# Two graph layers on one core: the attention weight as the larger of two exponentials instead of the exponential of a sum

## The reference

```python
def layer0(A, X, W, b):                       # X: normalised, rectified x
    idx = first 25 neighbours of each node by number
    agg = X[idx].max(axis=neighbours)          # and 0, where a node has 25 or fewer
    return relu(concat([X, agg]) @ W + b)

def layer1(inp, adj, W, a):
    h = inp @ W
    s1, s2 = h @ a[:256], h @ a[256:]
    e = leaky_relu(s1[:, :, None] + s2[:, None, :], negative_slope=0.4)
    att = softmax(where(adj > 0, e, -1e20), axis=1)
    return gelu(att @ h)

x = x + layer0(adj, relu(layernorm(x)), W0, b0)
x = x + layer1(relu(layernorm(x)), adj, W1, a)
```

## Time and profile before

| | us |
|---|---|
| median of three runs | 4289.62 |
| the three runs | 4287.83 to 4291.81 |
| the profiled execution | 4290.73 |
| its span on the core | 4288.9 |
| DVE busy | 3346.5 |
| POOL busy | 3107.7 |
| PE busy | 2657.1 |
| ACT busy | 1947.6 |

### The profile page before, as it was taken

One profiled execution on the slowest core, in us unless ns is written; L12 is line 12 of the kernel. 1 busy time (PEld: TensorE's weight loads), 2 busy tenths in 40 slices (PEclk: granted clock), 3 DMA queues, 4 the chain that ended last, 5 costly groups with the idle time before them and its releaser, 6 DMA issues. The chain is left out here.

```text
span 4288.9 us, 43562 instructions
## 1 busy us (share of the span) xinstructions
PE 2657.1 (62%) x13568; PEld 2016.8 (47%) x13568; DVE 3346.5 (78%) x7253; ACT 1947.6 (45%) x2108; POOL 3107.7 (72%) x3205
## 2 busy tenths in 40 slices
PE   2333356666666666675676666666666666666669
PEld 2222234554445454454454554455445554454547
DVE  5666689966898669986799767996689876998656
ACT  4223255532665236642366335553255532664146
POOL 5777777777777777777777777777777777777730
PEclk8555557677777777777767777777776777677779
DMA  6555556666666766666666766666666666566531
GB/s 216 166 167 173 174 183 216 209 221 212 208 213 206 232 212 197 218 221 223 203 216 204 226 222 206 213 199 225 213 211 217 210 225 218 188 218 202 172 114 55
DMA packets 412749, 860.09 MB, mean 201 GB/s; under 512 B 67299, under 2 KB 248422, under 8 KB 396134
## 3 DMA queue, kind: packets, MB, share of 16 engines
q0 software_dynamic: 153600, 419.64, 32.0%
q1 hardware_dynamic: 258918, 437.67, 30.2%
HBM read 714.43 MB, written 142.61 MB: 200 GB/s over the span
## 5 line engine op out<-in xcount | busy, mean ns | idle before, releaser
L410 POOL DMA_INDIRECT gb<-h_table,idx x3200 | 3107.0, 971 | 1009.2 <-issue 962.2
L965 PE MATMUL ps_av<-hz,lk 128*128 128x256 f32 x3712 | 1136.1, 474 | 179.1 <-DVE hz L805 179.1
L965 PEld LDWEIGHTS ps_av<-hz,lk 128*128 128x128 f32 x3712 | 891.4, 247 | 418.9 <-issue 256.6
L724 DVE TENSOR_REDUCE hl<-gb 128x256 f32<-128x3328 f32 x128 | 740.8, 5787 | 401.6 <-DMA gb<-h_table,idx 401.2
L724 DVE TENSOR_REDUCE gb<-gb 128x256 f32<-128x3328 f32 x128 | 748.5, 5847 | 10.9 <-DMA gb<-h_table,idx 10.9
L1018 PE MATMUL ps_t<-cf,hl 128*128 128x128 f32 x512 | 121.1, 382 | 694.2 <-DVE hl L724 694.2
L1023 PE MATMUL ps_l<-w,hcat 128*128 128x256 f32 x1024 | 461.1, 628 | 86.5 <-ACT hcat L538 86.5
L538 ACT COPY hcat<-ps_t 128x512 f32<-128x512 f32 x128 | 74.9, 585 | 864.9 <-PE ps_t L1018 864.5
L1036 PE MATMUL ps_t<-cf,y 128*128 128x128 f32 x256 | 72.2, 375 | 586.7 <-ACT y L551 586.7
L1018 PEld LDWEIGHTS ps_t<-cf,hl 128*128 128x128 f32 x512 | 79.3, 192 | 740.8 <-issue 740.8
L426 ACT ACTIVATE sg<-ps_c 128x2048 bf16<-128x2048 bf16 x128 | 240.1, 1876 | 410.3 <-PE ps_c L942 399.3
(11 more groups left out here) (128 smaller groups left out, 3555.9 us busy)
## 6 DMA issues: line engine op xcount, KB each, us to landing
ad<-in_adj SPq DMA_DIRECT2D x128, 1024.0 KB
p_rest<-lk SPq DMA_DIRECT2D x112, 512.0 KB, 3.4
lk<-p_rest SPq DMA_DIRECT2D x112, 512.0 KB, 3.9
gb<-h_table,idx POOLq DMA_INDIRECT x3200
edges_t<-stage SPq DMA_DIRECT2D x32, 1024.0 KB, 7.1
edge<-edges_t SPq DMA_DIRECT2D x64, 512.0 KB, 7.0
xl<-in_x SPq DMA_DIRECT2D x128, 128.0 KB
hl<-h_table SPq DMA_DIRECT2D x128, 128.0 KB
```

Of the source, the lines that this page charges most:

```text
L410: pool.indirect_dma_start(gb[c][:, s + (c > 0), :], None, table[tb], bass.IndirectOffsetOnAxis(idx[u][:, k:k + 1], 0)).then_inc(gathered[c ...
L724: V.tensor_reduce(dst, gb[c][:, :, :].rearrange("p k c -> p c k"), AX.X, ALU.max).then_inc(maxed[c], 1)
L965: ins = T.matmul(accumulator(k), lk_of(jj, u, drain)[:, k * P:(k + 1) * P], hz[jj][:, :], start=False, stop=False)
```

## The change

The leaky rectifier is the larger of x and 0.4 x, and the exponential grows with its argument; so the weight is the larger of two exponentials. ACT now computes exp(val + s2 + bias) into `lk`, and exp(0.4 val + bias) in place over `val` (`exps`). DVE takes the larger of the two in pieces of 512 and sums them with an accumulator per piece, `z_p` (`item_max`); `item_rows` sums the four. Both biases must stand before the exponentials, so `item_bounds` runs per item, right behind its values, with one instruction more, and `take_s2` moves ahead of the first values. What waited for `exp_ready` (PE, the store, `item_rows`) or `leaky_ready` (the next values in the same tile) now waits for `p_ready`, the maximum on DVE. `BLOCKED` becomes a power of two.

```diff
@@ ACT
-            def relu_part(i, j, jj, u, drain):
-                act.wait_ge(S["val_ready"], firsts(i) + 1)
+            def exps(i, j, jj, u, drain):
+                act.wait_ge(S["bounds_ready"], firsts(i) + 1)
                 act.wait_ge(S["av_done"], i - 2 if drain else i)
                 act.wait_ge(p_stored[jj], min(firsts(i) // 2, (NB - 1) * PAIRS) * 16)
-                nc.scalar.activation(lk_of(jj, u, drain)[:, :], val[jj][:, :], ACT.Relu, scale=1 - SLOPE,
-                                     bias=s2p[:, bass.ds(j, 1)]).then_inc(S["relu_ready"], 1)
-
-            def exp_part(i, j, jj, u, drain):
-                act.wait_ge(S["leaky_ready"], firsts(i) + 1)
-                bias, q = nb[:, bass.ds(j, 1)], lk_of(jj, u, drain)
-                nc.scalar.activation(q[:, :], q[:, :], ACT.Exp, bias=bias, accum_out=za[:, bass.ds(j, 1)]
-                                     ).then_inc(S["exp_ready"], 1)
+                nc.scalar.activation(lk_of(jj, u, drain)[:, :], val[jj][:, :], ACT.Exp, bias=nb[:, 1, bass.ds(j, 1)])
+                nc.scalar.activation(val[jj][:, :], val[jj][:, :], ACT.Exp, scale=SLOPE, bias=nb[:, 0, bass.ds(j, 1)]
+                                     ).then_inc(S["exps_ready"], 1)
...
-                if rest and not drain:
-                    exp_part(it - 2, j2, 0, 1 - u, drain)
                 if rest:
-                    relu_part(it - 1, j1, 1, 1 - u, drain and t > 0)
-                if rest and drain:
-                    exp_part(it - 2, j2, 0, 1 - u, drain)
+                    exps(it - 1, j1, 1, 1 - u, drain and t > 0)
...
-                if rest and not (drain and new):
-                    exp_part(it - 1, j1, 1, 1 - u, drain)
...
-                    relu_part(it, j, 0, u, drain)
-                if rest and drain and new:
-                    exp_part(it - 1, j1, 1, 1 - u, drain)
+                    exps(it, j, 0, u, drain)
@@ DVE
-            def item_bounds(o, i, j):
-                dve.wait_ge(S["val_ready"], firsts(i) + 2)
+            def item_bounds(o, i, j, jj):
+                dve.wait_ge(S["val_ready"], firsts(i) + 1)
...
+                dve.wait_ge(order, n)
+                V.tensor_tensor(nb[:, 1, bass.ds(j, 1)], nb[:, 0, bass.ds(j, 1)], s2p[:, bass.ds(j, 1)], ALU.add
+                                ).then_inc(S["bounds_ready"], 1)
...
-                    ins = V.scalar_tensor_tensor(out=q[:, p:p + PIECE], in0=val[jj][:, p:p + PIECE], scalar=SLOPE,
-                                                 in1=q[:, p:p + PIECE], op0=ALU.mult, op1=ALU.add)
-                ins.then_inc(S["leaky_ready"], 1)
+                    k = p // PIECE
+                    ins = V.scalar_tensor_tensor(out=q[:, p:p + PIECE], in0=q[:, p:p + PIECE], scalar=1.0,
+                                                 in1=val[jj][:, p:p + PIECE], op0=ALU.mult, op1=ALU.max,
+                                                 accum_out=z_p[:, jj, k:k + 1])
+                ins.then_inc(S["p_ready"], 1)
...
-                    dve.wait_ge(S["exp_ready"], firsts(i) + 1)
+                    dve.wait_ge(S["p_ready"], firsts(i) + 1)
+                    n = o.mark(V.tensor_reduce(za[:, bass.ds(j, 1)], z_p[:, jj, :], AX.X, ALU.add))
+                    dve.wait_ge(order, n)
                     n = o.mark(V.reciprocal(rz[:, bass.ds(j, 1)], za[:, bass.ds(j, 1)]))
```

More of the change, by code:

```diff
@@ L46 @@
 SLOPE = 0.4
-BLOCKED = 1e30
+BLOCKED = 2.0 ** 100
 PIECE = 512
@@ L153, in graph_layers @@
         m_a = sb("m_a", [P, 2, 2], fp32)
-        nb = sb("nb", [P, TILES], fp32)
+        nb = sb("nb", [P, 2, TILES], fp32)
+        z_p = sb("z_p", [P, 2, N // PIECE], fp32)
         za = sb("za", [P, TILES], fp32)
@@ L774, in item_value @@
                 ins.then_inc(S["val_ready"], 1)
-            def item_bounds(o, i, j):
-                dve.wait_ge(S["val_ready"], firsts(i) + 2)
+            def item_bounds(o, i, j, jj):
+                dve.wait_ge(S["val_ready"], firsts(i) + 1)
                 dve.wait_ge(order, o.n)
-                n = o.mark(V.tensor_reduce(m_t[:, :], m_p[:, :, :], AX.X, ALU.max))
+                n = o.mark(V.tensor_reduce(m_t[:, 0:1], m_p[:, jj, :], AX.X, ALU.max))
                 dve.wait_ge(order, n)
-                o.mark(V.tensor_scalar(m_a[:, 1, :], m_t[:, :], -SLOPE, None, ALU.mult))
-                n = o.mark(V.scalar_tensor_tensor(out=m_a[:, 0, :], in0=m_t[:, :], scalar=SLOPE - 1,
-                                                  in1=s2n[:, bass.ds(j, 2)], op0=ALU.mult, op1=ALU.add))
+                o.mark(V.tensor_scalar(m_a[:, 1, 0:1], m_t[:, 0:1], -SLOPE, None, ALU.mult))
+                n = o.mark(V.scalar_tensor_tensor(out=m_a[:, 0, 0:1], in0=m_t[:, 0:1], scalar=SLOPE - 1,
+                                                  in1=s2n[:, bass.ds(j, 1)], op0=ALU.mult, op1=ALU.add))
@@ L785, in item_bounds @@
                 dve.wait_ge(order, n)
-                o.mark(V.scalar_tensor_tensor(out=nb[:, bass.ds(j, 2)], in0=m_a[:, 0, :], scalar=0.0,
-                                              in1=m_a[:, 1, :], op0=ALU.min, op1=ALU.add))
-            def item_leaky(o, i, jj, u, drain):
+                n = o.mark(V.scalar_tensor_tensor(out=nb[:, 0, bass.ds(j, 1)], in0=m_a[:, 0, 0:1], scalar=0.0,
+                                                  in1=m_a[:, 1, 0:1], op0=ALU.min, op1=ALU.add))
+                dve.wait_ge(order, n)
@@ L791, in item_leaky, with item_max @@
+                V.tensor_tensor(nb[:, 1, bass.ds(j, 1)], nb[:, 0, bass.ds(j, 1)], s2p[:, bass.ds(j, 1)], ALU.add
+                                ).then_inc(S["bounds_ready"], 1)
+            def item_max(o, i, jj, u, drain):
                 q = lk_of(jj, u, drain)
-                dve.wait_ge(S["relu_ready"], firsts(i) + 1)
+                dve.wait_ge(S["exps_ready"], firsts(i) + 1)
                 for p in range(0, N, PIECE):
-                    ins = V.scalar_tensor_tensor(out=q[:, p:p + PIECE], in0=val[jj][:, p:p + PIECE], scalar=SLOPE,
-                                                 in1=q[:, p:p + PIECE], op0=ALU.mult, op1=ALU.add)
@@ L847, in step @@
                         take_s1(o, b)
+                        take_s2(o, b)
+                        dve.wait_ge(S["s_copied"], b)
                     if not sweep:
                         item_value(o, it, j, 0, drain)
+                        item_bounds(o, it, j, 0)
                 if old and drain and not before:
-                    item_leaky(o, it - 1, 1, 1 - u, drain)
+                    item_max(o, it - 1, 1, 1 - u, drain)
                 if old:
@@ L858, in step @@
                 if old and not drain and not before:
-                    item_leaky(o, it - 1, 1, 1 - u, drain)
-                if new and not t:
-                    take_s2(o, b)
+                    item_max(o, it - 1, 1, 1 - u, drain)
                 if words:
@@ L893, in step @@
                     item_value(o, it + 1, j + 1, 1, drain)
-                if new and sweep == 0:
-                    if not t:
-                        dve.wait_ge(S["s_copied"], b)
-                    item_bounds(o, it, j)
+                    item_bounds(o, it + 1, j + 1, 1)
                 if new and drain:
-                    item_leaky(o, it, 0, u, drain)
+                    item_max(o, it, 0, u, drain)
                 if old and t:
```

10 lines of the change are left out of this document (4 added, 6 removed).

## The result

| | us |
|---|---|
| before, median of 4 runs | 4290.28 (4287.83 to 4291.81) |
| after, median of 4 runs | 4321.42 (4316.75 to 4326.44) |
| ratio, 95% interval | 1.0072 (1.006 to 1.0084) |
| profiled execution of after, and its span | 4319.31, 4317.5 |

The change makes the kernel 31 us slower, 0.7%. The forecast was 13 us slower (4303): the direction is right, but the size is less than half of the loss. The time lies above the forecast's own range of 4290 to 4317 and inside the wider one of 4280 to 4330. The two spans differ by 4317.5 - 4288.9 = 28.6 us.

What follows compares the result with a forecast made beforehand. POOL sets the pace until the drain, with DVE as full in attention steps. 4290.7 us plus 12 uncovered DVE time plus 1.9 drain, less 1.1 for the median, gave 4303; own range 4290 to 4317, wider 4280 to 4330.

Steps and rivals of the forecast that it cites:

- The size of the addition: DVE in attention steps: bounds, sum and maximum add 1.5 us per step, 10.5 us per round.
- a halved maximum: Rival on DVE: each maximum piece takes twice 0.61 us, giving 4561 us; chance 8%.
- what of it is covered: Attention steps: existing DVE waits absorb all but 1.8 of the added 10.5 us per round, leaving some 12 us.
- I count the 6.8 us of landing waits as covered: Seven attention steps of a round: DVE's 6.8 us of waits for gathers to land absorb added work.
- because the landings come sooner: Reason for that cover: SP's store and loads go out some 11 us earlier, away from the second chunk's last gathers.
- Of the 3.8 us of waits for PE I count half: DVE's waits for layer 0's matmul: 1.9 us per round covered, as the second exponential precedes ACT's copy feeding it.
- accumulator reads that don't overlap: Maximum pieces on DVE: unhidden reads would cost 0.64 us per attention step, 27 us more in all, partly covered.
- POOL's waits for DVE, forecast at some 30 us: Sign of being right: POOL's waits for DVE rise from 16.2 us to some 30.
- I count no wait: DVE's maximum: an item's exponentials on ACT end ahead of it, so no wait is added.
- a sign of being wrong: Listed among the signs against the forecast: a new wait of DVE for the exponentials; no size given.
- The drain: End of the kernel: the rate stays, but PE's opening moves 1.9 us later, between 0 and 4.
- The store moved as forecast: SP, second item: its store waits for DVE's maximum instead of ACT's exponential and goes out about 11 us earlier.
- faster: Rival: accumulator reads between pieces let POOL's gathers through, up to 50 us; with half, 4271 us; chance 12%.

Runs made afterwards that it cites:

- b_bound: The kernel before with one bound per graph instead of one per item, the values keeping their unread accumulators; 4291.94 us, ratio 1.0004.
- b_extra: The kernel before with idle chains of dependent small DVE instructions, 1.4 us per attention step, added where the change adds work; 4305.1 us, ratio 1.0031.
- a_nob: The changed kernel without row-maximum bounds, biases from a constant with one small instruction per item; 4279.67 us, ratio 0.9975.
- a_split: The changed kernel with ACT's copy hcat between the second item's two exponentials instead of behind both; 4302.91 us, ratio 1.003.
- a_store: The changed kernel with the second item's store on SP held until layer 0's h1t of the step is copied; 4322.67 us, ratio 1.0071.
- a_late8: The changed kernel with the last item's maximum moved behind the first chunk's reduction in step t = 8 alone; 4323.12 us, ratio 1.0078.
- b_read: The kernel before with an accumulator on its combination, whose sum nobody reads; 4291.16 us, ratio 0.9998.
- a_one: The changed kernel with each item's maximum as one 2048-column instruction, whose accumulator is the whole sum; 4418.05 us, ratio 1.0302.
- b_glob: The kernel before with one bound per graph and the values as a plain addition without accumulators; 4324.21 us, ratio 1.007.

## Why the prediction was right in direction and short in size

The bound was read rightly. POOL sets the pace of the kernel before (`b_bound`), DVE stands just under it in the attention steps, and added DVE time there comes out at POOL (`b_extra`, `a_nob`).

The size of the addition was right: 10.5 us per round were forecast, about 10.0 were measured. The maximum takes 684 ns per piece, so the rival of a halved maximum did not happen. The Trainium skill's rule weighed there (Vector Engine (DVE) Microarchitecture Reference, "Points that are easy to get wrong"), half throughput with two SBUF sources that aren't bf16, does not agree with this trace: two fp32 tiles in SBUF take 684 ns with an accumulator and 690 without.

**The step that failed is "what of it is covered": "I count the 6.8 us of landing waits as covered".** The 6.8 us were read from one round, and it was richer than most: the mean over seven rounds is 40.4 / 7 = 5.8. And 1.9 per round stayed, of the 13.0 us in all 11.3 at the end of t = 1 in rounds 2 to 7. The step t = 0 ahead of it brings little lateness along, since DVE waits for gathers within it (at the first chunk, in five of these six rounds of the changed kernel). So only the addition of one step, 1.4 us, can fill the waits of t = 1, and it meets layer 0's product first: over rounds 2 to 7 that wait went from 6.1 us to none over 0.3, and the landing wait only from 14.1 to 11.3. These 8.9 us are about six times 1.4. The landing waits of all later steps vanished in these rounds. `a_split` keeps 2.1 per round, nearly all in the same place. So 3.9 were covered, not 6.8, which is 2.9 us per round more loss; the smaller addition (0.5 less) and the next term (0.5 more) cancel, and 1.8 becomes 4.6. One of its two reasons was wrong besides: "because the landings come sooner" did nothing (`a_store`).

The term beside it hid a second mechanism. "Of the 3.8 us of waits for PE I count half" names the second exponential ahead of the copy that feeds the matmul, and its size came out near, 10.0 / 7 = 1.4 us covered per round against 1.9. But it was written as a discount on a cover, and is a cost of its own: with the copy in between all of these waits can be filled (`a_split`, `b_extra`), and some 18 of the 31 us go. I priced the wait that was there instead of following the order of ACT from `hz` around to `x`. The two mechanisms of the loss are thus some 12 to 17 us of DVE time (12 from what `a_split` still loses, up to 17 from what `b_extra` loses) and the rest, some 14 to 19 us, of ACT's order. Counted in the traces' steps t = 1 to 7 alone, ACT's order is 15.2 of 32.5 us.

That the time lies inside the range of 4280 to 4330 is luck. The range was stretched above 4317 for accumulator reads that don't overlap; they do overlap here (pieces follow at 0.61), and the time went there for the two reasons above. POOL's waits for DVE, forecast at some 30 us, came to 58.7.

"I count no wait" for the exponentials failed as read: 12.9 us of waits at the maximum, 8.5 of them at t = 8 and the rest in the drain. Such a wait was named as a sign of being wrong, but it is not what cost the time: moving the maximum at t = 8 gained nothing (`a_late8`).

The drain: PE opens at 4189.74, 46.6 us behind the last gather, where the forecast had 47 and the kernel before 45.3. From the timeline of PE, as in the earlier trace rows:

```profile
4189.74 1.88 PE L996 MATMUL ps_av<-zeros 1*128 1x512 bf16 x4 [6.17 <-ACT go L502]
```

It moved by 1.3 us instead of 1.9. The store moved as forecast, from SP's timeline, as in the earlier trace rows: it now follows the row store by 0.42 us, where it was 11.74.

```profile
1676.17 0.32 SPq L338 DMA_DIRECT2D x_rows<-x  x1
1676.59 0.56 SPq L287 DMA_DIRECT2D p_rest<-lk  x1
1677.19 0.43 SPq L242 DMA_DIRECT2D edge<-edges_t  x1
```

Of the rivals, "faster" had a true part. The gathers beside the maximum are shorter than beside the combination, on POOL's timeline, as in the earlier trace rows:

```profile
1788.32 1.28 POOL L411 DMA_INDIRECT gb<-h_table,idx  x1 [1.72 <-DVE gb L711]
...
1792.41 1.13 POOL L411 DMA_INDIRECT gb<-h_table,idx  x1 [0.30 <-issue]
```

1.13 us stands beside the maximum, 1.40 beside the combination; summed over all gathers that overlap them, the time above 0.946 us fell from 43 to 25 us. POOL's busy time fell by 11. That case needs 25, half of its 50 (its sum took 20), and its condition, an addition on DVE of under 1 us per step, did not hold. Its reason, the reads between pieces, is not borne out either (`b_read`); what shortens these gathers stays open.

## What to carry to other kernels

A cover is a sum over every round and step it is spent in: read the waits of all rounds, and set each wait against the work that is added ahead of it in its own step. When two halves of a job are put together on an engine, look at what small copy stood between them and who waits for it; here one copy of 0.56 us behind a 2-us activation cost about half of the loss (18 of 31 us in the medians, 15 of 32 in the steps t = 1 to 7). And follow the loop through all engines (`hz`, product, exponentials, copy, product, `x`) before pricing a wait as if it stood alone.

## What the runs showed of the hardware that was not expected

An indirect gather on POOL was held by DVE's passes over two SBUF tiles until 0.8 us behind their end: 2.83 us beside one pass of 2048 columns (`a_one`), 5.42 us beside eight passes of 512 without accumulators (`b_glob`), against a median of 0.946. That is not always so: beside the four passes of the combination before, which follow each other without a break as well, one took 1.40 us. What decides was not found. Fewer and longer DVE instructions, with 31 us less DVE time, made the kernel 97 us slower (`a_one`, 4418 against 4321). Accumulators whose results nobody reads came with 32 us less at one place (`b_bound` against `b_glob`, where the instruction changed too) and with nothing at another (`b_read`).
